# Another queue for the pair bias, and another place for the factor's round trip, in the gated attention block

## What is computed

```python
# layernorm(x): m = mean(x), v = var(x); (x - m) / sqrt(v + eps)
x = x + tanh(g_xattn[0]) * xattn(layernorm(x), ctx_1024, ctx_1024, fside_Bx16xSxS2_0, ...)
x = x + tanh(g_ffn[0]) * ffn(layernorm(x), ...)

# xattn(q, k, v, attn_bias, ...); each projection is x W' + b + 2 (x A') B'
scores = einsum('bqhd,bkhd->bhqk', qh * 16**-0.5, kh) + attn_bias
out = einsum('bhqk,bkhd->bqhd', softmax(scores), vh)

# ffn: of 8 experts the one with the largest logit
h = gelu(einsum('th,ehi->tei', xf, W1) + b1); y = einsum('tei,eih->teh', h, W2) + b2
out = take_along_axis(y, argmax(softmax(xf @ Wg + bg)))
```

## Time and profile before

| | us |
|---|---|
| median of 3 runs | 2015.0 |
| lowest and highest | 2010.71 and 2022.11 |
| the profiled execution, its own time | 2017.96 |
| its span from first to last instruction | 2016.1 |
| attention stage, start to about | 1744 |
| of it SP's sends, first to last | 5.8 to 1697.7 |
| expert stage | 1744 to 2016 |

### The profile page before, as it was taken

The page is one execution under the profiler, slowest core; times in us unless marked ns, Lnnn a source line. Parts: engine busy times, 40 slices in busy tenths (PEclk is TensorE's granted clock), DMA queues, the critical chain, the costliest instruction groups (busy, mean ns, idle before and its releaser), DMA issues.

```text
span 2016.1 us, 45866 instructions
## 1 busy us (share of the span) xinstructions
PE 1390.3 (69%) x12568; PEld 1158.6 (57%) x12568; DVE 974.1 (48%) x5961; ACT 772.7 (38%) x1660; POOL 997.8 (49%) x1051
## 2 busy tenths in 40 slices
PE   5656666676766666766656666767665666999998
PEld 3445545554655455555545555656554555788887
DVE  3334445443544444444444444545444444756555
ACT  1334434343433343443333343434333343533333
POOL 2334545554545445554445444545445445655555
PEclk7778878888877788877878887878787888999999
DMA  4454556555556565566556555665555654688896
GB/s 113 125 119 126 132 126 132 101 130 131 131 111 123 127 122 113 124 131 131 111 122 131 129 114 116 130 131 131 125 111 129 127 115 107 214 289 281 276 284 215
DMA packets 156795, 289.27 MB, mean 143 GB/s; under 512 B 36836, under 2 KB 72166, under 8 KB 156544
## 3 DMA queue, kind: packets, MB, share of 16 engines
q1 hardware_dynamic: 142992, 252.02, 55.1%
q0 software_dynamic: 12624, 34.62, 4.6%
q10 hardware_dynamic: 1056, 1.39, 0.2%
HBM read 251.89 MB, written 36.98 MB: 143 GB/s over the span
## 4 chain that ended last, share of the span: by engine, by line
DMA 69%; PE 14%; SPq 9%; issue 6%; DVE 1%; ACT 0%; POOLq 0%; POOL 0%; DVEq 0%; ACTq 0%
DMA rs_dram<-x2n 68%; PE bank L788 6%; PE bank L802 6%; SPq L402 5%; SPq L366 2%; PE bank L776 1%; DMA x_sb<-in_x 1%; DMA RS<-rs_dram 1%; DVE sc L1042 1%; SPq L356 0%; PE bank L595 0%; PE bank L629 0%; PE bank L620 0%; SPq L384 0%; SPq L379 0%
## 5 line engine op out<-in xcount | busy, mean ns | idle before, releaser
L1042 DVE CUSTOM_DVE_ANT_0 sc<-bank,sc 128x128 f32<-128x128 f32 x2048 | 443.9, 286 | 264.3 <-PE bank L595 133.7
L484 POOL TENSOR_TENSOR sc<-sc,rowmax 128x1024 f32<-128x1024 f32 x256 | 480.0, 1896 | 156.9 <-DVE rowmax L1042 148.7
L595 PE MATMUL bank<-KT,QT 32*128 32x256 f32 x2048 | 195.6, 509 | 476.0 <-DVE QT L1101 443.9
L595 PEld LDWEIGHTS bank<-KT,QT 32*128 32x128 f32 x2048 | 119.7, 238 | 511.5 <-DVE QT L1101 373.3
L506 POOL TENSOR_SCALAR ve<-mv 128x2 f32<-128x2 f32 (+1 forms) x135 | 31.5, 233 | 674.3 <-DVE mv L1065 649.9
L620 PE MATMUL bank<-cst,sc 128*128 128x128 f32 x2048 | 291.6, 289 | 1.2 <-issue 1.2
L886 ACT ACTIVATE PT<-bank 128x512 f32<-128x512 f32 x512 | 281.6, 604 | 17.6 <-PE bank L620 14.1
L620 PEld LDWEIGHTS bank<-cst,sc 128*128 128x128 f32 x2048 | 243.2, 149 | 35.0 <-issue 34.7
L1052 DVE BATCH_NORM_STATS2 st<-x_sb 128x6 f32<-128x256 f32 x128 | 53.7, 419 | 399.6 <-DMA x_sb<-in_x 399.5
L852 ACT ACTIVATE QT<-QT,cst 128x256 f32<-128x256 f32 x128 | 58.0, 501 | 444.8 <-DVE QT L1101 444.8
L645 PE MATMUL bank<-XT,wq 128*128 128x256 f32 x512 | 148.0, 439 | 115.0 <-DVE rowmax L1042 114.5
(11 more groups left out here) (148 smaller groups left out, 2157.1 us busy)
## 6 DMA issues: line engine op xcount, KB each, us to landing
sc<-in_bias SPq DMA_DIRECT2D x256, 512.0 KB
w_sb<-in_w SPq DMA_DIRECT2D x69, 257.0 KB, 3.9
CT<-in_w SPq DMA_DIRECT2D x69, 256.0 KB, 4.0
xg<-rows_dram SPq DMA_DIRECT2D x63, 272.0 KB, 3.9
x_sb<-in_x SPq DMA_DIRECT2D x128, 128.0 KB, 11.1
CT<-in_ctx_in SPq DMA_DIRECT2D x64, 256.0 KB
XT<-in_x_turned SPq DMA_DIRECT2D x64, 256.0 KB
RS<-rs_dram SPq DMA_DIRECT2D x128, 64.0 KB
```

The source lines that it names most:

```text
L484: nc.gpsimd.tensor_tensor(s, s, m, ALU.subtract).then_inc(sub_ok, 1)
L595: ins = mm(b_s[j][:, 2 * P * c:2 * P * c + 2 * P], QT[rows, pair, c, P * sq:P * sq + P], KT[rows, pair, c, sq].rearrange("p e k -> p (e k) ...
L1042: ins = nc.vector.tensor_tensor_reduce(out=s, in0=b_s[q][:, P * (h % 4):P * (h % 4) + P], in1=s, scale=1.0, scalar=LOWEST, op0=ALU.add, op ...
```

## The change

Three things change. SP's step now sends and spreads the factor first, before the other loads; the wait for the send to land therefore stands ahead of `CT`, `x_sb` and `XT`. Only in the steps up to -2 does the pair still come last. SP no longer loads the bias, nor waits for `tr_ready`. ACT loads it: the first three sequences' ahead of everything but the weights, and that of sequence s + 3 in its step s, behind the exponentials of quarters 2 and 3, which have themselves waited for `tr_ready`, and ahead of the queries' bias.

```diff
             def step(i, k):
                 behind = seq(i, k, -4)
-                if behind and not (isinstance(i, int) and k < 0):
+                if behind and not (isinstance(i, int) and k < -1):
                     send_scale(behind)
+                    spread_scale(behind)
                 t = seq(i, k, -6) if k > FIRST else None
...
-                if behind and isinstance(i, int) and k < 0:
+                if behind and isinstance(i, int) and k < -1:
                     send_scale(behind)
-                if behind:
                     spread_scale(behind)
-                t = seq(i, k, -3)
-                if t:
-                    if t.reached(4):
-                        sp.wait_ge(tr_ready, t.n(4, -12))
-                        sp.nop(nofuse=True)
-                    if not t.reached(1):
-                        sp.wait_ge(s_w["k"], 16)
-                    for h in range(0, HEADS, 8):
-                        sp.dma_start(sc[:, t.slot(4), h * P:(h + 8) * P],
-                                     bias[t.n(), :, h * P:(h + 8) * P]).then_inc(bias_in[t.slot(4)], 16)
...
+            def load_bias(t):
+                for h in range(0, HEADS, 8):
+                    act.dma_start(sc[:, t.slot(4), h * P:(h + 8) * P],
+                                  bias[t.n(), :, h * P:(h + 8) * P]).then_inc(bias_in[t.slot(4)], 16)
+
+            for n in range(3):
+                load_bias(At(0, n, U))
             act.wait_ge(s_id, 16)
...
                 if prev and not scored:
                     probs(prev, 2)
                     probs(prev, 3)
+                t = seq(i, k, -3)
+                if t and t.reached(3):
+                    load_bias(t)
                 if qry and qry.slot(2) == 0:
                     queries(qry)
```

## The result

| | before | after |
|---|---|---|
| median, us | 2013.1 (2010.71 to 2022.11) | 1958.3 (1951.88 to 1968.59) |
| ratio | 1 | 0.9725, 95% interval 0.9672 to 0.9777 |
| span of the profiled execution | 2016.1 | 1954.8 |

The changed kernel is 2.75% faster, 55 us. Forecast were 233 us and a range of 1700 to 1900. The direction was right and the size four times too large.

What follows compares the result with a forecast made beforehand. SP's send round trip was taken to bound each step, 13.35 us. Trip 9.3, open issues 2.0 and 0.1 gave 11.4, over 126 steps 246 us gained; less 10 for DVE's stops and 3 at the start: 1782 us, range 1700 to 1900.

Steps and rivals of the forecast that it cites:

- What bounds the kernel: Attention stage: SP's wait for its send sets the beat, 13.35 us a step, with a round trip of 11.65 us.
- The bias leaves SP's queue: SP's send no longer stands behind 1 MB of bias; its round trip falls from 11.65 us toward a floor of 8.93.
- ACT's phase: ACT starts the bias after its last exponentials, 0.35 us after SP's send, so its data fill the trip's idle part.
- The trip of 9.3 us: SP's send round trip after the change, taken near the floor of 8.93 us, with 0.3 to 0.4 for queued loads.
- The open part of 2.0 us: SP's issues between landing and next send: 1.25 us in odd steps, 2.6 in even, mean 1.9, plus 0.1 for waking.
- rival D: SP held by `x2_ok` or `rs_ok` of a late DVE: up to 60 us more, 1842 us; 0.79 together with the forecast.
- The start: Three biases, 3 MB, go out ahead of SP's first loads and delay the first sends by 3 us.
- C: Rival: the trip falls to its floor and the engines limit, 10.9 or 10.4 us a step, 1665 to 1725 us; chance 0.05.
- The engines' floor: Attention stage: the engines need about 9 us a step, 10.4 with DVE's stops, below the forecast step of 11.4.
- sign of being wrong: Two signs set beforehand: the trip staying above 10.5 us (first term), or SP waiting over 50 us for DVE (slack).
- A: Rival: ACT's phase drifts, bias often falls on spread and send; step 12.5 to 13.1 us, 1920 to 2000 us; chance 0.09.
- B: Rival: another queue does not shorten the trip, 11.65 us; step 14.0 to 14.6 us, slower at 2100 to 2180; chance 0.05.

Runs made afterwards that it cites:

- e7: e1 with the send's 128 numbers 512 bytes apart in DRAM and the spread reading `x`, so the factor is left out: 1292.7 us, one run.
- e10: e1 with the factor going through a row in one partition of SBUF instead of DRAM, nothing left out: 1299.5 us, ratio 0.6619 to the kernel before.
- e1: The changed kernel with SP's old order restored and the bias still loaded by ACT: 1809.2 us, ratio 0.9291 to the kernel before.
- e8: The changed kernel with `CT` and `XT` issued between send and spread, `x_sb` still behind the spread: 1852.0 us, ratio 0.9451 to the kernel before.
- e4: The changed kernel with seven eighths of the bias left out from the fifth sequence on: 1783.2 us, ratio 0.9141 to the kernel before.
- e3: The changed kernel with the factor in its own tile, computed before GpSimd's wait for the scatter: 1880.0 us, ratio 0.9629 to the kernel before.
- e6: e1 with the factor in its own tile, computed before GpSimd's wait for the scatter: 1760.8 us, ratio 0.8989 to the kernel before.
- e12: The kernel before with the factor going through a row in one partition of SBUF instead of DRAM: 1312.6 us, ratio 0.669 to the unaltered kernel before.
- e11: The changed kernel with the factor going through a row in one partition of SBUF instead of DRAM: 1397.8 us, ratio 0.7124 to the kernel before.

## Why the prediction was wrong

**What bounds the kernel** held. It was SP's send, and e7 and e10 show it to its full extent. That the second, idle part of the trip "belongs to the send itself" held too. I did not ask why 128 small writes should take 6 us, and so took a trip of 8.93 us for a floor; e10 has 5.8 us, and is a third faster than the kernel before.

**The bias leaves SP's queue** held in sign: 7.1% by itself, from a trip of 8.6 us (e1). That is near the floor of 8.93 that I had read in the earlier trace rows. ACT's phase was right in kind: the bias starts behind the send, though 3.4 us behind it and not 0.35, and about one time in twelve ahead of it.

**The trip of 9.3 us** is the first term that failed, by 0.9 us: 10.2 measured, 9.3 behind `x_sb` alone and 11.1 behind `CT`, `x_sb` and `XT`. For these loads I had put "half or less" of 1.0 us. They cost 1.8 us in every second step, as they move when the bias joins them; e8 and e4 each take one of the two away, and each brings the trip back to 8.4 to 9.0. I had used the row of 16.25, a send behind spread and `x` with an idle machine, for a queue of more than three times the bytes. A trip of 10.2 us was the range's upper end, 1895 us: this term alone would not have left the range.

**The open part of 2.0 us** is the second: 2.6, worth 76 us over 126 steps, and with it the time left the range. The issues themselves are what I had added up (e3, without the other wait, has 1.96). The other 0.6 is SP's wait for GpSimd's factor. I had followed the factor from DVE to SP, and named `rs_ok` in rival D, but as a consequence of DVE's stops. What made it late in ordinary steps was GpSimd's wait for the scatter of the step before. It was in the code, and in the trace of before worth 24 us. In the changed kernel, as in e1, the scatter is issued 1.1 us behind the send (median; 4.6 in the kernel before), and the scatter was then counted as landed 9.8 us after its issue, 0.9 us after the spread of the same step; in e10 4.6 us after it.

**The start**: I allowed 3 us. The second send left at 25.0 us instead of 16.25, 8.8 us later, the first one having taken 17.7 us among the 3 MB of bias:

```profile
5.19 1.05 SPq L356 DMA_DIRECT2D rs_dram<-x2n  x1
22.91 0.33 SPq L366 DMA_DIRECT2D RS<-rs_dram  x1
...
25.00 0.65 SPq L356 DMA_DIRECT2D rs_dram<-x2n  x1
...
1632.69 0.34 SPq L356 DMA_DIRECT2D rs_dram<-x2n  x1
```

The sum closes with these. From second to last send pass 1607.7 us, 12.76 a step: gain 126 x (13.345 - 12.76) = 73.7. Less 8.8 at the start, and 3.7 after the last send (322.1 against 318.4 us), this is 61.2; the spans differ by 61.3. The forecast had 246, less 13.

**Slips in the forecast's own figures.** The range's lower end is said to take the trip to 8.93 us, but its 0.65 us a step is more than the 0.37 that this gives; by it the end would be 1735 us. C's times come by the same sum to about 1646 to 1719, not 1665 to 1725. Neither touches the outcome.

**The engines' floor** of 9 us, and 10.4 with DVE's stops, was wrong, though it decided nothing: e10 runs a step in 7.6. PE's 8.5 us of a step had been read at a clock of 0.81; kept busy it had 0.99, and took 7.4 (929.8 us by 126).

**What held**: `x_sb` lands in 4.6 us (4 to 5 forecast), DVE waits 528 us for it (400 to 550), SP 1144 us for the send (1150), ACT's queue carries 135.6 MB (135), the granted clock is 0.83 (0.81 or more), and ACT's two issues cost nothing that shows. The trip stayed below 10.5 us, the sign set for the first term, and SP's wait for DVE below 50 us, so neither sign of being wrong spoke. None of these tells one cause from another: the wait of SP would be 1144 us by several sums.

**The rivals.** The time is that of A, 1920 to 2000, but A's cause, a drift of ACT's phase, is the smaller part of it: 9 in 116 sends at 13.1 us instead of 10.0 are 0.2 us a step, of the 1.4 us by which the step was missed. B's rule from the Trainium skill ("DMA: Bandwidth & Descriptors"), that another queue brings no bandwidth, agrees with the runs as far as it goes: with the row in place the other queue is worth 1%. In e1 it was worth 7%, not as bandwidth, but because a wait of SP stood behind the bias. The second half of the rule from the Trainium skill, that a completion count waits for earlier writes of its engine in any queue, fits the scatter that counts as landed just after the send. That it is this mechanism and not another was not tested.

Not settled: why send to spread grows by 0.7 (e3) and 1.9 us (e6) when the factor has its own tile, most of it before the first landing; and why sixteen writes into the same 64 bytes are slow.

## What to carry to other kernels

A queue's round trip that ends every step must be taken apart before anything is put around it: how long it takes alone, and why. Here the bias's other queue was worth 7%, the new order cost 5%, and the cause of the trip, sixteen 4-byte writes into each 64 bytes of DRAM, was worth 33% by itself (e12). What stands ahead of such a send counts by its bytes still moving, from all queues (e8, e4), and a wait moved ahead of independent loads stands in the open (e11: 98 us). Whoever makes a ring faster should look, for each engine on it, at what it waits for one step back: waits worth 24 us in the old trace can be 558 in the new.

## What the runs showed of the hardware

128 writes of 4 bytes from 128 partitions into 512 adjacent bytes of DRAM took 8.4 to 11.5 us from send to spread, by what else moved, of which 5.8 to 7.1 us lay between the first and the last landing. The same writes 64 or 512 bytes apart, writes of 64 bytes side by side, or the same 4 bytes side by side into one partition of SBUF have 1.3 to 1.5 us there, and let the kernel of e1 run in 1288 to 1299.5 us instead of 1809 us. While the adjacent writes were under way other transfers were held up as well: the scatter landed 9.8 us after its issue (4.6 in e10), and a packet of the bias took 0.75 us in the stretch of 789 to 795.8 us (0.17 in e10 over the stage); the DMA share of the stage was 0.73 for 127 GB/s, against 0.71 for 213 GB/s in e10. Reading one partition's row for all 128 partitions did not show in the time (e10 against e7). The same kernel took 2013 us in one measurement and 1953 to 1961 us in later ones on two chips.
